# Attention stage of a graph network: TensorE subtracts the running maximum from the scores while turning them

## The reference

```python
h = relu(layernorm(x))
hh = h.reshape(n, 12, 64)
ft = einsum('nhd,ed->nhe', hh, W_fc)
a1 = einsum('nhd,hd->nh', ft, attn_l);  a2 = einsum('nhd,hd->nh', ft, attn_r)
e = leaky_relu(a1[src] + a2[dst], 0.2)
m = segment_max(e, dst)
ee = exp(e - m[dst])
alpha = ee / segment_sum(ee, dst)[dst]
agg = segment_sum(alpha[:, :, None] * ft[src], dst)
x = x + relu(einsum('nhd,ed->nhe', hh, W_res) + agg)
```

## Time and profile before

| | us |
|---|---|
| median of 3 runs | 1844.84 |
| lowest and highest | 1842.23, 1847.53 |
| the profiled execution | 1838.35 |
| its span | 1836.5 |

### The profile page before, as it was taken

How to read it: one execution, slowest core, us unless ns; L and a number is a source line. 1 busy time by engine, 2 the same in 40 slices (tenths; PEclk the granted TensorE clock), 3 DMA queues, 4 the chain that set the end, 5 groups by cost and what they waited for, 6 DMA issues and landing times. The chain is left out here.

```text
span 1836.5 us, 43411 instructions
## 1 busy us (share of the span) xinstructions
PE 1317.4 (72%) x13383; PEld 855.2 (47%) x13384; DVE 1094.9 (60%) x1947; ACT 759.4 (41%) x2383; POOL 1236.2 (67%) x1297
## 2 busy tenths in 40 slices
PE   6357777778777857888788888872676676666665
PEld 4224444444444534555555555541454444444443
DVE  7724444445444524555555555543888888888886
ACT  6601111111111111222222222223788888888885
POOL 3167777777777457777777777607777777777760
PEclk9978899899989978999999999986878888888887
DMA  9679999999999669999999999919999999999991
GB/s 266 245 253 333 353 349 337 329 333 336 333 331 331 230 237 333 363 356 371 370 362 358 352 363 372 335 66 330 314 339 347 345 350 347 355 352 346 351 315 61
DMA packets 139994, 585.27 MB, mean 319 GB/s; under 512 B 30615, under 2 KB 32751, under 8 KB 139945
## 3 DMA queue, kind: packets, MB, share of 16 engines
q0 software_dynamic: 100272, 497.49, 75.7%
q1 hardware_dynamic: 32563, 67.72, 10.7%
q10 hardware_dynamic: 7110, 19.43, 2.8%
HBM read 534.42 MB, written 50.12 MB: 318 GB/s over the span
## 5 line engine op out<-in xcount | busy, mean ns | idle before, releaser
L704 POOL DMA_INDIRECT ring_c<-table,slot_c x834 | 795.7, 954 | 307.0 <-issue 286.9
L1202 POOL DMA_INDIRECT ring<-table,slot x417 | 414.7, 995 | 140.5 <-issue 116.3
L757 ACT ACTIVATE slot_c<-units 128x8 int32 (+1 forms) x104 | 21.7, 210 | 790.6 <-DMA ring_c<-table,slot_c 738.4
L1347 ACT ACTIVATE ring<-ring,weight x1152 | 279.0, 336 | 0.6
L1609 DVE TENSOR_TENSOR ring<-ring,ps_w 128x3120 f32 x72 | 242.7, 3399 | 18.0 <-ACT ps_w L1327 18.0
L1451 PE MATMUL ps_acc<-ring,hot_f 128*32 128x195 f32 x3136 | 178.3, 375 | 87.2 <-DVE ring L1609 86.0
L956 DVE TENSOR_TENSOR hots<-iota,units 128x256 f32<-128x256 bf16 x102 | 42.9, 428 | 301.6 <-PE ps_sum0a L904 118.4
L899 PE MATMUL ps_yb<-weights,sum_tb 128*128 128x512 f32 (+1 forms) x576 | 193.3, 492 | 2.9 <-ACT weights L791 0.8
L899 PE MATMUL ps_ya<-weights,sum_ta 128*128 128x512 f32 (+1 forms) x576 | 189.9, 486 | 0.0
L1451 PEld LDWEIGHTS ps_acc<-ring,hot_f 128*32 128x32 f32 x3136 | 105.2, 123 | 148.4 <-DVE ring L1609 111.1
L899 PEld LDWEIGHTS ps_yb<-weights,sum_tb 128*128 128x128 f32 x576 | 108.1, 191 | 84.0 <-issue 71.1
(11 more groups left out here) (296 smaller groups left out, 1950.6 us busy)
## 6 DMA issues: line engine op xcount, KB each, us to landing
ring_c<-table,slot_c POOLq DMA_INDIRECT x834
table<-weights SPq DMA_DIRECT2D x25, 396.0 KB, 5.3
table<-nodes SPq DMA_DIRECT2D x25, 384.0 KB
table<-nodes ACTq DMA_DIRECT2D x25, 384.0 KB, 5.4
turned_table<-weights SPq DMA_DIRECT2D x25, 384.0 KB
nodes<-in_x ACTq DMA_DIRECT2D x24, 384.0 KB
turned_g<-turned_table SPq DMA_DIRECT2D x24, 384.0 KB
out_x<-nodes SPq DMA_DIRECT2D x24, 384.0 KB
```

Source lines behind the costliest of these rows:

```text
L704: eng.indirect_dma_start(out=ring[:, t * QH + k, :], out_offset=None, in_=table, in_offset=bass.IndirectOffsetOnAxis(ap=slot[t][:, k:k + 1 ...
L757: eng.activation(slot[t][:, :], units[:, ds(q, 1), t * QH:(t + 1) * QH + t].rearrange("p a c -> p (a c)"), ACT.Copy).then_inc(slot_ready[t ...
L1202: eng.indirect_dma_start(out=ring[:, b * RB + at * FROW:b * RB + (at + 1) * FROW], out_offset=None, in_=table3, in_offset=bass.IndirectOff ...
L1347: last = eng.activation(head, head, ACT.Copy, scale=weight[:, c, h:h + 1])
```

## The change

The maximum of score and slope is now written to `score`, a buffer in SBUF with one column more for the carried maximum, and the forward scan reads it there. PE no longer waits for a finished difference. It waits for `z_made` and puts the scores through an identity with five matmuls in place of five transposes, turns the next hot matrix, waits for `top_made`, and adds five matmuls of the scanned maximum with `minus`, a 48x48 identity times -1, on top of the first five in PSUM. DVE's subtraction (L1580) and its semaphore go. `minus` is made once at the start of the stage.

```diff
--- before.py
+++ after.py
@@ -1048,7 +1048,8 @@
             a2_blk = sb(st, "a2_blk", [P, UH])
             far_of = sb(st, "far_of", [P, UH])
             far = sb(st, "far", [P, 1])
-            score = sb(st, "score", [UH, WIN])
+            score = sb(st, "score", [UH, 1 + WIN])
+            minus = sb(st, "minus", [UH, UH])
             top = sb(st, "top_g", [UH, 1 + WIN])
             same = sb(st, "same_g", [UH, 1 + WIN], BF16)
             run = sb(st, "run", [UH, 1])
@@ -1089,7 +1090,6 @@
             z_made = sem(st, "z_made")
             z_max = sem(st, "z_max")
             top_made = sem(st, "top_made")
-            s_diff = sem(st, "s_diff")
             t_made = sem(st, "t_made")
             w_made = sem(st, "w_made")
             own_made = sem(st, "own_made")
@@ -1114,7 +1114,6 @@
             W0 = 3 * P
             given_w = ps_w[:, 0:UC * UH].rearrange("p (c r) -> p c r", r=UH)
             shared_w = ps_w[:, UC * UH:UC * UH + H]
-            with_carry = ps_s[0:UH, W0 - 1:W0 + WIN]
             ps_ht = ps_s[:, 0:UC * P // 2].bitcast(BF16)
             ps_e = ps_s[:, 512:512 + UC * UH].rearrange("p (c r) -> p c r", r=UH)
 
@@ -1424,12 +1423,16 @@
                         nu = units_of(j)
 
                         def visit(q, nth, left):
-                            eng.wait_ge(s_diff, q + 1)
+                            eng.wait_ge(z_made, q * 2 + 2)
                             eng.sem_inc(passed, 1)
                             for c in range(UC):
-                                last = eng.transpose(ps_e[:, c, :], score[:, c * P:(c + 1) * P], ident[0:UH, 0:UH])
+                                eng.matmul(ps_e[:, c, :], score[:, 1 + c * P:1 + (c + 1) * P], ident[0:UH, 0:UH], start=c == 0, stop=True, skip_group_check=True)
+                            by_parity(eng, eng.snap(q % 2), lambda b: turn_hot(q + 1, 1 - b))
+                            eng.wait_ge(top_made, q + 1)
+                            eng.sem_inc(passed, 1)
+                            for c in range(UC):
+                                last = eng.matmul(ps_e[:, c, :], top[:, 1 + c * P:1 + (c + 1) * P], minus[:, :], start=False, stop=True, skip_group_check=True)
                             last.then_inc(t_made, 1)
-                            by_parity(eng, eng.snap(q % 2), lambda b: turn_hot(q + 1, 1 - b))
                             with eng.If(nth < 1):
                                 eng.sem_inc(r_hot, 1)
                                 eng.sem_inc(r_all, 1)
@@ -1492,7 +1495,8 @@
                     eng.memset(run[:, :], 0.0)
                     eng.memset(nil[:, :], 0.0)
                     eng.memset(same[:, :], -BIG)
-                    eng.memset(with_carry[:, 0:1], 0.0)
+                    eng.memset(score[:, 0:1], 0.0)
+                    eng.tensor_scalar(minus[:, :], ident[0:UH, 0:UH], -1.0, None, ALU.mult)
                     eng.memset(far[:, :], -FAR)
                     eng.memset(far_of[:, :], 0.0)
                     eng.memset(a2[:, NT, :], 0.0)
@@ -1568,16 +1572,16 @@
                                 carry(q)
                             eng.wait_ge(z_low, q + 1)
                             eng.wait_ge(c_chain, q + 1)
-                            eng.tensor_copy(with_carry[:, 0:1], run[:, :]).then_inc(z_made, 1)
-                            eng.tensor_tensor(window(0, WIN), window(0, WIN), top[:, 1:1 + WIN], ALU.max).then_inc(z_made, 1)
+                            eng.tensor_copy(score[:, 0:1], run[:, :]).then_inc(z_made, 1)
+                            eng.tensor_tensor(score[:, 1:1 + WIN], window(0, WIN), top[:, 1:1 + WIN], ALU.max).then_inc(z_made, 1)
                             eng.wait_ge(z_made, q * 2 + 2)
                             eng.wait_ge(same_in, q * (16 * US) + 16 * US)
-                            eng.tensor_tensor_scan(top[:, :], same[:, :], with_carry, -BIG, ALU.add, ALU.max).then_inc(z_max, 1)
+                            eng.tensor_tensor_scan(top[:, :], same[:, :], score[:, :], -BIG, ALU.add, ALU.max).then_inc(z_max, 1)
                             eng.wait_ge(z_max, q + 1)
                             back = slice(None, None, -1)
                             eng.tensor_tensor_scan(top[:, 0:WIN][:, back], same[:, 1:1 + WIN][:, back], top[:, 0:WIN][:, back], top[:, WIN:1 + WIN], ALU.add, ALU.max).then_inc(top_made, 1)
                             eng.wait_ge(top_made, q + 1)
-                            eng.tensor_tensor(score[:, :], window(0, WIN), top[:, 1:1 + WIN], ALU.subtract).then_inc(s_diff, 1)
+                            eng.sem_inc(passed, 1)
                             with eng.If(nth < 1):
                                 eng.sem_inc(r_chain, 3)
                                 for s in (r_diff, r_lift, r_done):
```

## The result

The changed kernel took 1866.24 us (median of 4, 1865.15 to 1870.28) against 1844.22, a ratio of 1.0115 with a 95% interval of 1.0095 to 1.0135: slower by 22 us. The forecast of 1847.0 named the likeliest case and it didn't come. The time lies in the range (1840 to 1868), near its end, but for the reason of rival B, to which I had given 0.09.

A forecast was written before the change was run, and what follows sets the result against it. The prediction took ACT's laying and cast to bound the attention visit, with 0.85 us spare on the maximum's path. First visits -1.5 and POOL +3.7 gave +2.2 us on the median 1844.84: 1847.0 us, range 1840 to 1868.

The forecast's parts named there:

- the likeliest case: Attention stage: POOL unaffected and only the first visits change, 1843 us; forecast with it, within 5.5 us, chance 0.54.
- rival B: PE late for ACT with the second matmul batch, deciding from 1.6 us a batch; 1860 to 1875 us, chance 0.09.
- rival A: POOL's gathers delayed behind L1575 and L1578; up to 1863 us if let in between, else 1857 to 1891; chance 0.28.
- What bounds: Attention visit: ACT's laying and cast lead to the exponential; the maximum's path has 0.85 us spare, so removing L1580 gains nothing.
- The matmul batch's price: PE: five matmuls, ten instructions, 0.96 to 1.48 us from L1430, taken as 0.96; upper end 2.31; cost in 23 visits 0.
- The sum by the factor four: PE batch priced by the skill's transpose factor: 1.92 us, result at 1543.1, 0.7 us late, +16 us.
- PE's arrival: PE starts the first batch 0.44 us after L1451, at 1538.39, and stands at the second wait at 1540.1 (1540.9 low clock).
- The clock: PE's second batch ends at 1541.2, or 1542.4 at the lower granted clock, against ACT's need at 1542.35; cost 0.
- The first two visits: Start of the stage, where L1327 waited for L1430: PE arrives one wait earlier, -1.5 us together, once.
- POOL: Gathers reading inside L1575, now with two SBUF inputs, wait for its end: stretch 1.16 us a visit, +3.7 us, ends 0 to +20.
- L1575 on SBUF: DVE's forward scan reading the score from SBUF: 1.54 in place of 1.48 us, +0.06 us, inside the 0.85 us spare.
- The sum: -1.5 us for the first visits plus 3.7 for POOL gives +2.2, set against the median 1844.84: 1847.0 us.

The follow-up runs named there:

- e7: The kernel before with ACT laying 12 of its 16 pieces, a quarter of the attention's result left out; 1837.16 us, ratio 0.9967.
- e9: The kernel before with ACT's cast of the hot matrix moved behind the two exponentials; 1833.52 us, ratio 0.9932.
- e4: The changed kernel with both PE batches as five transposes each, the second overwriting the first, so the maximum is not subtracted; 1845.69 us, ratio 1.0010.
- e8: The kernel before with five matmuls for its transposes and, three times a visit, five unread f32 filler matmuls on PE; 1879.61 us, ratio 1.0198.
- e3: The kernel before with its five PE transposes as five f32 matmuls, the scan still reading PSUM; 1862.04 us, ratio 1.0077.
- e11: The changed kernel with its first batch in transpose mode with the matmuls' flags, so the second batch adds to it; 1849.38 us, ratio 1.0042.
- e2: The kernel before with one more DVE maximum written to SBUF and the forward scan reading it there, PE's transposes kept; 1848.74 us, ratio 1.0026.
- e1: The kernel before with one more DVE maximum written to SBUF and read by nobody, the scan still reading PSUM; 1846.06 us, ratio 1.0006.
- e5: The changed kernel with only its first batch as five plain transposes, each with its own start, so the subtraction is not formed; 1849.04 us, ratio 1.0028.

## Why the prediction was right and wrong

That 1866 lies in the range is luck. The range reached to 1868 for rival A with gathers let in between; the loss came by rival B, and the sum had 0 for it.

- **What bounds: right.** ACT's laying and cast set the visit (e7, e9), the maximum's path had room, and L1580 off it was worth nothing (e4).
- **The matmul batch's price: the step that failed.** I took 0.96 us from L1430's shape and called L1378 the upper end, 2.31 us, because it moves 128 columns. It is 1.31 at the high clock and 2.37 at the low, 0.131 and 0.237 us an instruction. L1378's 0.231, a mean over instructions most of which ran at the low clock, was the right row for that level. With 128 weight columns an f32 matmul's instruction costs nearly the same for 48 moving columns as for 128: e8's filler, ten instructions with 128, took 1.35 us at the high clock and 2.46 at the low, the batch L1430 of e3 with 48 took 1.28 and 2.34. The transposes, one instruction a block, hid that. The Trainium skill ("TensorE: Matmul & The Clock Gate", Terms), which calls transpose mode four times as fast for f32, was nearer than my row: the same five blocks took 0.48 us as transposes and 1.28 as matmuls at the high level, 0.74 and 2.34 at the low, so 2.7 and 3.2 times. (The sum by the factor four, worked as the others, is 1543.0, 0.6 us late and +15 us, not 1543.1, 0.7 and +16.)
- **PE's arrival: failed.** "With 0.44 us for the border, as ACT shows": PE needed 1.59 us (1555.07 to 1556.67) in this visit and 1.31 in e11. Before, the wait for DVE covered it. With the border and 1.70 for the first batch PE began the second batch 0.76 us after L1582's end, where the forecast had 0.15 us and PE there 0.1 us ahead.
- **The clock: weighed in the text and left out of the sum.** I worked out both levels, wrote "before 1542.35 (even with it)", and took the better one. The second batch was at the high level throughout in 6 of 25 visits.
- **The first two visits: wrong in sign.** I forecast -1.5 us. PE comes late at new code in the second (3.40 us after its last unit, against 3.80 before), and then has three pieces of work to do where it had one: 5.3 us. The first interval between exponentials grew from 22.46 to 26.69 us, +4.2, the second from 22.75 to 23.58. In e4, with transposes only, the first is 25.54, so most of the +4.2 is not the matmuls' price.
- **POOL: the mechanism right, the price not refuted.** Stretches grew from 0.77 to (1027 - 950) x 17 = 1.31 us a visit, where 1.16 was forecast; the second gather's 0.32 us was forecast as 0.33. Against the term of +3.7 us stand 2.7 (e2 over e1, inside noise) and at most 4.6 (e4), both with smaller stretches, and the 3.7 us of L1294 in the change itself, whose cause is open.
- **L1575 on SBUF:** 1.49 us, not 1.54.
- **The sum.** From the kernel before, by medians and by ratios: the change with transposes only is +1 or +2 us (e4), with the second batch as matmuls +5 to +8 (e5, e11), with both +22 or +21. The forecast had 0 for both batches. Rival B was priced at 1860 to 1875 and came at 1866.

## What to carry to other kernels

Price an f32 matmul by the row of another f32 matmul with as many weight columns, at both granted clocks, and never by a transpose; where work is split around a wait, the part ahead of the wait has to fit too, with the engine's own loop border in front of it. Work taken off an engine that isn't on the path buys nothing, and its replacement is paid as far as it goes beyond what the path had to spare, here 0.85 us. The spare itself was worth more than the change: moving one cast behind the instruction that everybody waits for gave 11 us.

## What was not expected of the hardware

- The granted clock fell in every visit of e8, though PE was busy 359 of 400 us there against 273 before; the means over 1400 to 1800 us are 0.79 and 0.84. So filler work did not raise it. Busy time does not order the kernels either (e3: 283 us, 0.83; the change: 308 us, 0.81; e11: 292 us, 0.85), and it is itself longer at the low clock. The Trainium skill ("TensorE: Matmul & The Clock Gate", Part 1) ties the low level to a PE that was idle. In e8 PE had been idle for 1.20 us ahead of the filler and 0.51 us ahead of the batch in which the clock fell, and it then worked 2.00 of 2.00 us at 0.50; the kernel before, where PE was idle for 3.07 us ahead of L1430, has the higher mean. That shorter pauses keep the clock up is not borne out here, and what lowers it stays open.
- In the looped visits of the changed kernel and e11, PE needs 1.3 to 1.9 us, mostly 1.3 to 1.6, from the last matmul of one pass to the first of the next, ACT 0.44.
- A DVE instruction with both inputs in SBUF delays a gather that starts inside it (it took 1.58 us in place of 0.95 in e2's rows, 2.09 in the changed kernel at 1555.28), and a gap of 0.03 us between two such instructions lets one gather through.
